# Plain steps of an ODE kernel: earlier fp16 tanh, low-half products last, next injections among them

## What is computed

```python
def _mlp(y, W1, b1, W2, b2, W3, b3):
    h = jnp.tanh(y @ W1.T + b1)
    h = jnp.tanh(h @ W2.T + b2)
    return h @ W3.T + b3
k1 = f(y); k2 = f(y + dt / 2 * k1); k3 = f(y + dt / 2 * k2); k4 = f(y + dt * k3)
y = y + dt * (k1 + 2 * k2 + 2 * k3 + k4) / 6
```

## Time and profile before

| | us |
|---|---|
| median of 3 runs | 2888.99 (2886.65 to 2889.01) |
| the profiled execution: its run | 2888.1 |
| its span, first to last instruction | 2886.3 |
| plain steps within it | 2143 to 2877 |

### The profile page before, as it was taken

How to read it: one execution, slowest core, us unless ns; L and a number is a source line. 1 busy time by engine, 2 the same in 40 slices (tenths; PEclk the granted TensorE clock), 3 DMA queues, 4 the chain that set the end, 5 groups by cost and what they waited for, 6 DMA issues and landing times.

```text
span 2886.3 us, 207890 instructions
## 1 busy us (share of the span) xinstructions
PE 2805.1 (97%) x81958; PEld 2402.4 (83%) x81958; DVE 2359.0 (82%) x13272; ACT 1549.3 (54%) x10124; POOL 726.9 (25%) x1346
## 2 busy tenths in 40 slices
PE   7789999999999999999999999999999999999999
PEld 3478888888888888888888887888889999999998
DVE  5778888888888888888888887888888888888887
ACT  6455555555555555555554444444445555555555
POOL 5222332332332332332332000111112222222222
PEclk9789999999999999999999999999999999999999
DMA  3000000000000000000000000000000000000000
GB/s 118 0 12 11 13 12 11 13 12 11 14 12 11 14 12 11 14 12 11 14 11 8 1 0 1 0 0 0 0 17 0 0 0 0 0 0 0 0 0 15
DMA packets 21982, 28.21 MB, mean 10 GB/s; under 512 B 4384, under 2 KB 12896, under 8 KB 21544
## 3 DMA queue, kind: packets, MB, share of 16 engines
q1 hardware_dynamic: 21928, 27.48, 3.1%
HBM read 25.24 MB, written 2.23 MB: 10 GB/s over the span
## 4 chain that ended last, share of the span: by engine, by line
PE 93%; DVE 3%; ACT 2%; issue 1%; DMA 0%; SPq 0%; DVEq 0%; ACTq 0%; POOLq 0%; POOL 0%
PE PSUM L681 22%; PE PSUM L687 21%; PE PSUM L888 17%; PE PSUM L742 12%; PE PSUM L672 5%; PE PSUM L884 4%; PE PSUM L779 1%; DVE PSUM L1395 1%; PE PSUM L844 1%; PE PSUM L849 1%; PE PSUM L708 1%; ACT HA L1072 1%; PE PSUM L712 1%; PE PSUM L749 1%; PE PSUM L510 1%
## 5 line engine op out<-in xcount | busy, mean ns | idle before, releaser
L1395 DVE TENSOR_REDUCE PSUM<-PSUM 128x32 f32<-128x64 f32 x2912 | 624.9, 232 | 96.8 <-PE PSUM L687 51.1
L681 PEld LDWEIGHTS PSUM<-HA,RL 128*128 128x128 f16 x11648 | 396.3, 96 | 205.8 <-ACT HA L1072 196.4
L1073 ACT ACTIVATE PSUM<-PSUM 128x32 f32<-128x32 f32 x2912 | 562.1, 194 | 0.0
L1072 ACT ACTIVATE HA<-PSUM 128x32 f16<-128x32 f32 x1456 | 287.6, 198 | 469.2 <-DVE PSUM L1395 469.1
L1072 ACT ACTIVATE HB<-PSUM 128x32 f16<-128x32 f32 x1456 | 287.9, 199 | 466.0 <-DVE PSUM L1395 466.0
L681 PE MATMUL PSUM<-HA,RL 128*128 128x16 f16 x11648 | 512.1, 170 | 15.3 <-ACT HA L1072 7.6
L681 PE MATMUL PSUM<-HB,RLU 128*128 128x16 f16 x11648 | 511.0, 170 | 3.6
L422 POOL TENSOR_TENSOR G<-G 128x512 f16<-128x512 f32 x256 | 296.6, 1159 | 682.9 <-ACT G L1045 682.9
L687 PE MATMUL PSUM<-HA,RH 128*128 128x32 f16 x11648 | 466.0, 177 | 0.0
L687 PE MATMUL PSUM<-HB,RHU 128*128 128x32 f16 x11648 | 464.8, 177 | 0.0
L681 PEld LDWEIGHTS PSUM<-HB,RLU 128*128 128x128 f16 x11648 | 393.6, 96 | 46.7 <-ACT HB L1072 1.9
(11 more groups left out here) (307 smaller groups left out, 6686.7 us busy)
## 6 DMA issues: line engine op xcount, KB each, us to landing
G<-scores SPq DMA_DIRECT2D x64, 256.0 KB, 3.1
N<-in_x SPq DMA_DIRECT2D x8, 256.0 KB, 4.7
NHL<-in_w SPq DMA_DIRECT2D x1, 2048.0 KB, 10.1
STF<-in_w SPq DMA_DIRECT2D x1, 2048.0 KB, 14.6
out<-W2HL SPq DMA_DIRECT2D x8, 256.0 KB, 2.4
G<-in_r SPq DMA_DIRECT2D x1, 1024.0 KB, 5.3
R1K<-in_r SPq DMA_DIRECT2D x1, 256.0 KB, 2.9
R3F<-in_r SPq DMA_DIRECT2D x1, 256.0 KB, 5.4
```

Of the source, the lines that this page charges most:

```text
L681: mm(out[m // 2][:, 2 * B * (m % 2):2 * B * (m % 2) + B], lo[:, k, m], src[:, k, 0], start=False, stop=False)
L1072: A(hi[:, 2 * h:2 * h + 2, 0], src, ACT.Tanh, scale=1.0 / scale).then_inc(rk_hi, 1)
L1073: A(full, src, ACT.Tanh, scale=1.0 / scale).then_inc(rk_f, 1)
L1395: v.tensor_reduce(bank[:, SUM:SUM + 2 * B].rearrange("p (m b) -> p m b", m=2), bank[:, 0:4 * B].rearrange("p (m c b) -> p m b c", m=2, c=2 ...
```

## The change

SPLIT_ORDER is rewritten so that in every layer the eight `l` products come last (places 32 to 39). sp_p of group 0 is raised behind the last product of m = 0, 1 that is not an `l` (h30 at place 19); a new semaphore sp_all is raised behind the last `l` (l10). The fp16 tanh of m = 0, 1 waits for sp_p, so it reads sums without the low-half products; the full tanh waits for sp_all, and the low half, being the difference, takes up what the fp16 value lacks. The first `l` product waits until that fp16 tanh has read the sums. The fp16 tanh of m = 2 reads the first half of PAIRED, ahead of VectorE's reduce, which now waits for it. ScalarE takes the three fp16 tanhs first and then the full ones in the order of groups 0, 2, 1; VectorE reduces and subtracts in that order too. The next layer's opening (with the state products that used to stand ahead of it) is issued at place 36, ahead of the last four `l` products.

```diff
 SPLIT_ORDER = [(w[0], int(w[1]), int(w[2])) for w in (
-    "L11 L10 h00 L13 L00 h10 h11 h01 L01 L02 L12 h20 L21 L20 l10 l00 H12 l01 L32 h31 L30 h21 l11 l21 L31 H22 l20 "
-    "h30 H02 l30 l31 H32 L22 L03 H23 H33 H03 H13 L23 L33").split()]
+    "L01 h11 L10 L11 L00 L12 h10 h00 L02 L20 L23 h20 L21 h21 h01 L13 h31 L30 L31 h30 "
+    "L33 L32 L22 L03 H03 H13 H02 H12 H33 H32 H23 H22 l01 l31 l21 l11 l00 l20 l30 l10").split()]
+OPEN_NEXT_AT = 36
...
+                    if i == OPEN_NEXT_AT:
+                        open_next()
...
-                    ends = all(SPLIT_OF[m] != SPLIT_OF[b] for _, _, b in SPLIT_ORDER[i + 1:])
+                    if kind == "l" and not after_read:
+                        after_read = True
+                        pe.wait_ge(sp_hi[0], split_count(s, j, lay) + 1)
+                    rest = [(a, b) for a, _, b in SPLIT_ORDER[i + 1:] if SPLIT_OF[b] == SPLIT_OF[m]]
+                    ends = all((a == "l") != (kind == "l") for a, _ in rest)
...
                     if ends:
-                        t.then_inc(sp_p[SPLIT_OF[m]], 1)
+                        t.then_inc(sp_all if kind == "l" else sp_p[SPLIT_OF[m]], 1)
+
+            def open_second(s, j):
+                pe.wait_ge(rk_s, 4 * s + j)
+                split_inject(1, IDV, CI[:, 3], True)
+
+            def open_first(s, j):
+                if j == 1:
+                    pe.wait_ge(rk_hs, s)
+                    state_high()
+                if j == 2:
+                    state_low()
+                pe.wait_ge(rk_u, 4 * s + j + 1)
...
+                    split_layer(s, j, 0, RH2, RL2, HA, opening and j == 0, lambda: open_first(s, j))
+                    split_layer(s, j, 1, RHU[:, COEF_OF[j]], RLU[:, COEF_OF[j]], HB, False,
+                                lambda: open_second(s, j + 1))
...
-                        for g, ms in enumerate(SPLIT):
-                            act.wait_ge((sp_r if g else sp_p)[g], split_count(s, j, lay))
-                            sl = slice(ms[0], ms[-1] + 1)
-                            A(hi[:, sl, 0], SPLIT_SUM[lay][:, sl], ACT.Tanh, scale=1.0 / scale).then_inc(sp_hi[g], 1)
+                        act.wait_ge(sp_p[0], split_count(s, j, lay))
+                        A(hi[:, 0:2, 0], SPLIT_SUM[lay][:, 0:2], ACT.Tanh, scale=1.0 / scale).then_inc(sp_hi[0], 1)
+                        act.wait_ge(sp_p[1], split_count(s, j, lay))
+                        A(hi[:, 2, 0], PAIRED[lay][0][:, 0:B], ACT.Tanh, scale=1.0 / scale).then_inc(sp_hi[1], 1)
+                        act.wait_ge(sp_r[2], split_count(s, j, lay))
+                        A(hi[:, 3, 0], SPLIT_SUM[lay][:, 3], ACT.Tanh, scale=1.0 / scale).then_inc(sp_hi[2], 1)
+                        for g, done in ((0, sp_all), (2, sp_r[2]), (1, sp_r[1])):
+                            act.wait_ge(done, split_count(s, j, lay))
+                            sl = slice(SPLIT[g][0], SPLIT[g][-1] + 1)
                             A(SPLIT_FULL[lay][:, sl], SPLIT_SUM[lay][:, sl], ACT.Tanh, scale=1.0 / scale).then_inc(sp_f[g], 1)
...
-                            for g in (1, 2):
+                            for g, ready in ((2, sp_p[2]), (1, sp_hi[1])):
                                 ms = SPLIT[g]
-                                dve.wait_ge(sp_p[g], split_count(s, j, lay))
+                                dve.wait_ge(ready, split_count(s, j, lay))
...
-                            for g, ms in enumerate(SPLIT):
+                            for g in (0, 2, 1):
                                 dve.wait_ge(sp_f[g], split_count(s, j, lay))
```

More of the change, by code:

```diff
@@ L257, in build @@
         sp_p, sp_r, sp_hi, sp_f, sp_lo = ([sem(f"sp_{k}{g}") for g in range(3)] for k in ("p", "r", "hi", "f", "lo"))
+        sp_all = sem("sp_all")
         def split_count(s, j, lay):
@@ L866, in add_low, with split_layer @@
                     mm(PAIRED[0][m - 2][:, 0:B], IDU[:, :], both[:, m, 1], start=False, stop=False)
-            def split_layer(s, j, lay, hi, lo, src, opening):
-                waited = set()
+            def split_layer(s, j, lay, hi, lo, src, opening, open_next):
+                waited, after_read = set(), False
                 for i, (kind, k, m) in enumerate(SPLIT_ORDER):
+                    if i == OPEN_NEXT_AT:
+                        open_next()
                     if i == LOW_AT and lay == 1 and j in (0, 3):
@@ L887, in split_layer @@
                         half = src[:, k, 1 if kind == "l" else 0].unsqueeze(1).to_broadcast([128, copies, B])
-                        t = mm(repeated(1 - lay, m, B, copies), (lo if kind == "L" else hi)[:, k, m], half, start=False, stop=ends)
+                        t = mm(repeated(1 - lay, m, B, copies), (lo if kind == "L" else hi)[:, k, m], half, start=False,
+                               stop=ends, skip_group_check=kind == "l")
                     if ends:
-                        t.then_inc(sp_p[SPLIT_OF[m]], 1)
+                        t.then_inc(sp_all if kind == "l" else sp_p[SPLIT_OF[m]], 1)
@@ new lines, in open_second @@
+            def open_second(s, j):
[8 more added lines that the diff above has]
+                pe.wait_ge(rk_u, 4 * s + j + 1)
+                if j in (0, 3):
+                    open_high(UZ if j == 0 else BZ, UI if j == 0 else BI)
+                else:
+                    if j == 2:
+                        pe.wait_ge(x_bl, s - S_PLAIN + 1)
+                    split_inject(0, IDU, UI if j == 1 else IB, True)
@@ L892, in split_step @@
             def split_step(s, opening):
                 for j in range(4):
[L894 to L908, removed]
@@ L909, in split_step @@
-                    split_layer(s, j, 1, RHU[:, COEF_OF[j]], RLU[:, COEF_OF[j]], HB, False)
+                    split_layer(s, j, 0, RH2, RL2, HA, opening and j == 0, lambda: open_first(s, j))
+                    split_layer(s, j, 1, RHU[:, COEF_OF[j]], RLU[:, COEF_OF[j]], HB, False,
+                                lambda: open_second(s, j + 1))
+            open_second(S_PLAIN, 0)
             split_step(S_PLAIN, True)
@@ L1118, in _ @@
                 split_step(s, False)
+            act.wait_ge(sp_p[0], split_count(STEPS, 0, 0))
+            A(HA[:, 0:2, 0], SPLIT_SUM[0][:, 0:2], ACT.Tanh, scale=1.0 / SCALE_U).then_inc(sp_hi[0], 1)
             for i in range(OG):
```

## The result

| | before | after |
|---|---|---|
| median of the runs timed together, us | 2888.61 (2886.65 to 2889.01) | 2936.41 (2936.22 to 2936.50) |
| ratio after / before, 95% interval | | 1.0167 (1.0154 to 1.0180) |
| profiled execution, us (its span) | 2888.1 (2886.3) | 2936.5 (2934.7) |
| plain stage, first to last product, us | 734.0 | 783.6 |
| one plain step, median of the turns, us | 10.04 | 10.72 |

The change makes the kernel slower by 47.8 us, forecast 50 (2939 us). All of it lies in the plain stage: its first product issues at 2143.25 us before and 2142.50 after, its last at 2877.23 and 2926.09, so it is 49.6 us longer, 0.68 us in each of the 73 steps. The two profiled executions differ by 48.4 us, since the parts around it were 1.2 us shorter after the change.

What follows compares the result with a forecast made beforehand. TensorE's issue and waits bound the kernel, with l01's wait for the fp16 tanh setting the new layer cycle. Terms of 0.28 + 0.20 + 0.07 - 0.06 + 0.20 = 0.69 us over 73 steps gave 2939 us, range 2908 to 2978.

Steps and rivals of the forecast that it cites:

- ring, eight layers: From h30 through its tanh to l01 and on to the next h30: 1.255 to 1.26 us a layer, +0.28 a step.
- state products in the ring: Eight state products a step, moved between l01 and the next h30 where nothing waits beside them: +0.20 us a step.
- loop turn: PE's loop jump, half hidden before, now lies between l10 and L01 and counts in full: +0.07 us a step.
- openings of three matmuls: Two layers a step open with three matmuls, now between l01 and the next h30: -0.06 us a step.
- late consumers at place 36: Injections at place 36 wait for VectorE's operations behind the last subtraction, mainly in two layers: +0.20 us a step.
- The low halves: PE stands 0.06 us at H03 and 0.03 at H23 for them, under l01's wait: no cost.
- The tanh of m2: Without its sum, ready 0.41 us after l01 and wanted 0.55 after: no cost.
- PE dense: Rival: l01's wait is over when PE comes, a step takes 9.35 us, 2838 us in all; chance 0.07.
- VectorE held: Rival: subtractions stand a full 0.18 us apart, delaying l01 by 0.135; 3018 us, or 2977; chance 0.09.
- Only the ring grows: Rival: state products and consumers find cover after all, 0.29 us a step, 2910 us; chance 0.10.
- It does not do what it says: Rival: new waits are met early and late alike, the step stays within 10.05 us; chance 0.04.

Runs made afterwards that it cites:

- Runs 1: The changed kernel with two products, L02 and L23, moved from between l01 and h30 to just behind h30; 2919.52 us.
- run 4: The changed kernel with the next layer's injections and state products behind the last l product (place 40 instead of 36); 2926.09 us.
- the short ring: The changed kernel with injections at place 40 and L02, L23, L12, L13 moved behind h30, then at place 15; 2881.61 us, 0.9976 of the kernel before.
- Run 2: The changed kernel with its l products written to a bank nobody reads, so l01 has no wait; 2897.88 us.
- run 3: The changed kernel with the state products moved from place 36 to place 32, ahead of l01; 2928.39 us.
- run 6: The changed kernel with the fp16 tanh of m2 waiting again for its sum, which VectorE reduces first; 2944.32 us.

## Why the prediction was right, point by point

It named the bound, the new wait and the sum. Per step, by the layers' medians over the turns:

| term, us a step | forecast | measured |
|---|---|---|
| ring, eight layers | +0.28 | +0.25 (1.26 against 1.23) |
| state products in the ring | +0.20 | +0.21 (0.10 and 0.11) |
| loop turn | +0.07 | +0.19 (1.505 - 1.261 = 0.244, before 1.287 - 1.229 = 0.058) |
| openings of three matmuls | -0.06 | -0.05 |
| late consumers at place 36 | +0.20 | +0.08 |
| sum | 0.69 | 0.68 |

- *The ring.* From h30 to l01 the trace shows 0.46 us as forecast, 0.21 to the tanh and 0.25 back. Runs 1 and 4 and the short ring show that a plain layer is this wait and what stands from l01 to h30: 1.26, 1.21 and 1.16 us for products moved by two and by four. Run 2 shows that the wait is the change's own cost: without it 38.5 of the 47.8 us go, out of five of the eight layers.
- *The state products* cost what was forecast, and run 3 gives half of it back from place 32; the rest goes to the next late thing.
- *The low halves* under l01's wait cost nothing, shown by run 4. They stand a little less than forecast (0.04 at H03 and 0.01 at H23, forecast 0.06 and 0.03).
- *The loop turn is the term that was sized too small*, by 0.12. The prediction took over the 0.16 of standing from one turn of the kernel before (0.15 in the median) and half of it as hidden already; after, PE stands 0.26 - 0.025 = 0.235, and nothing hides it. The branch has no row in the views, but its record in the trace shows where the time goes: before, it starts at 2514.990 us, with eight products still to issue (the last at 2515.182), and most of its 0.21 us lies beside them. After, it starts at 2507.676, 0.18 after l01 is released (2507.496), and lasts until 2507.891, past the last product at 2507.797. From the branch's start to the first product behind it are 0.36 to 0.38 us in the median turn of every kernel compared here, so the price goes with how far ahead of the last product the branch starts: 0.19 us before, 0.14 in run 4, 0.12 after the change, 0.09 in run 2 and 0.075 in the short ring, for 0.17, 0.24, 0.26, 0.29 and 0.30 us from product to product. What holds the branch back is not settled. The four with the dearer turn have a wait that PE stands at within the last twelve products, and the kernel before has none there; but l01's wait by itself is not it, as run 2 takes that one away and the turn gets dearer, with PE standing at the injection.
- *The late consumers are the term that was sized too large*, by 0.12. The place and the layers were right (run 4 removes them, 0.08 a step), their size was not. Counted from l10's issue (2503.885 in the layer shown), the prediction had the first subtraction at 0.45; it starts at 0.42, as the full tanh is 0.18 long and the subtraction follows it by 0.03 instead of 0.05. The prediction then spaced the Vector operations by about 0.10; the last two of the subtractions and the first consumer come 0.08 apart, so that consumer starts at 0.69 instead of 0.75. The injections are some 0.04 and 0.05 late instead of 0.09 and 0.10. The lower bound of nothing was nearer than the value taken.
- The two misses have opposite signs and nearly the same size; the total of 47.8 against 50 is better than its parts, and that they cancel is luck.
- *The tanh of m2* was said to cost nothing, with 0.14 us to spare. That is borne out, and run 6 shows its other side: without this part the change would be 8 us slower.

The rivals: *PE dense* fell, since l01 stands for its tanh. *VectorE held* fell by the row of three subtractions in 0.35 us; one after the other, each for its whole length, they would have taken 0.19 + 0.165 + 0.165 = 0.52. The Trainium skill (VectorE: DVE Perf Modes, section "The DRAIN you can't avoid") has the next operation start only when the pipe is empty, unless it is not held. The trace agrees with the exception alone: two like subtractions in a row overlap by half, 0.081 apart and 0.165 long. *Only the ring grows* (2910) fell by the layers of 1.36 and 1.37. *It does not do what it says* fell by the step of 10.72.

One reading of the prediction was short: three layers of the kernel before are longer than plain ones, not two (1.307 and 1.298 with low injections, 1.287 with the turn, in the median). The low injections of j = 3 lie outside; the sum counts both openings, so it doesn't change.

What stays open: what PE stands for in the first pass through a loop body, and what holds the branch at the turn back.

## What to carry to other kernels

Starting a consumer early doesn't help when its producer must then wait until the consumer has read: count the new ring (the round trip, plus all that stands from the release to the next request), not the wait that disappears. Work that lay under the old wait is paid in full once that wait is gone, so it has to move under the new one: here the same early tanh went from 1.7% slower to 0.66% faster by moving products, state work and injections to the other side of the wait. A gain stops at the next late input, and in each layer that is another one, so read the layers one by one and not their mean.

## What was not expected of the hardware

- A turn of PE's loop has no fixed price: PE stood 0.15 us beyond a product in the kernel before, 0.235 after the change, and 0.27 in the short ring (0.297 from product to product), the more the less the branch starts ahead of the last product.
- In the first pass through a doubled loop body PE stood up to 0.94 us between two products; that ate the whole gain of half the turns in the kernel before. The change's body of one step has one such stand of 0.49 us.
- Subtractions of 16 columns on VectorE start 0.081 us apart though each lasts 0.165; behind a product that waited, the next one issues 0.038 us later instead of 0.025.
